# Head attention ahead of the first mixture in 32-row tiles, and values projected between the rows of the recurrent attention

## What is computed

```
# ffn0, ahead of its mixture: 16 heads of 8, batches of 64 tokens
Q = hs @ q_w + q_b; K = hs @ k_w + k_b; V = hs @ v_w + v_b
attn = softmax(Q[..., :8] @ K.T / sqrt(8)); ao = attn @ V
mla_out = concat(ao, 0) @ o_w + o_b          # the mixture's input
# attn1: 8 heads of 64
q, k, v = x @ Wq + bq, x @ Wk + bk, x @ Wv + bv
attn = softmax over heads of (q . k) * 64**-0.5
state = decay * state + (1 - decay) * attn * v     # over time
out = (q * state + sigmoid(q * aug)) @ Wo + bo
x = x + layernorm(out) * ln_scale + ln_bias
```

## Time and profile before

| | us |
|---|---|
| median of 3 runs | 1057.94 (1055.94 to 1062.13) |
| the profiled execution, its own time | 1060.44 |
| its span in the profile | 1058.7 |
| PE busy | 989.5 |
| DVE busy | 567.9 |
| ACT busy | 493.3 |
| POOL busy | 175.0 |

### The profile page before, as it was taken

How to read it: one execution, slowest core, us unless ns; L and a number is a source line. 1 busy time by engine, 2 the same in 40 slices (tenths; PEclk the granted TensorE clock), 3 DMA queues, 4 the chain that set the end, 5 groups by cost and what they waited for, 6 DMA issues and landing times. The chain is left out here.

```text
span 1058.7 us, 20860 instructions
## 1 busy us (share of the span) xinstructions
PE 989.5 (93%) x8710; PEld 814.5 (77%) x8710; DVE 567.9 (54%) x809; ACT 493.3 (47%) x696; POOL 175.0 (17%) x169
## 2 busy tenths in 40 slices
PE   8899999787789998899999999999999988959997
PEld 7788888664569995689999999999999966537554
DVE  4578776676634434665555555556564612176222
ACT  5677776252346653544545454544445421402221
POOL 2000000104304433011111111111111101320000
PEclk9899999899779999999999999999999999977999
DMA  5121110112013314021111111111130001988990
GB/s 163 45 66 45 48 45 3 27 34 64 1 51 92 96 40 159 4 78 40 41 41 40 40 40 40 40 40 40 40 119 0 1 1 33 292 287 222 300 303 20
DMA packets 55205, 81.47 MB, mean 77 GB/s; under 512 B 5073, under 2 KB 44578, under 8 KB 55138
## 3 DMA queue, kind: packets, MB, share of 16 engines
q1 hardware_dynamic: 55138, 80.49, 24.5%
HBM read 79.96 MB, written 0.52 MB: 76 GB/s over the span
## 5 line engine op out<-in xcount | busy, mean ns | idle before, releaser
L181 PE MATMUL ps<-f_pT_hi,f_cN_hi 128*128 128x256 f32 x512 | 145.4, 284 | 2.4 <-DVE f_pT_lo L1699 2.4
L181 PE MATMUL ps<-f_pT_hi,f_cN_lo 128*128 128x256 f32 x512 | 144.7, 283 | 0.0
L181 PE MATMUL ps<-f_pT_lo,f_cN_hi 128*128 128x256 f32 x512 | 144.7, 283 | 0.0
L1446 ACT ACTIVATE e_pr<-ps,e_negmax 128x1024 f32<-128x1024 f32 x64 | 71.5, 1118 | 129.8 <-DVE e_negmax L1451 127.5
L1699 DVE TENSOR_TENSOR f_pT_lo<-ps,f_pT_hi 128x1024 fp32r<-128x1024 f32 x64 | 78.3, 1224 | 81.7 <-ACT f_pT_hi L1647 81.6
L181 PE MATMUL ps<-e_cT_hi,e_qb_hi 128*128 128x512 f32 x256 | 105.6, 413 | 0.0
L1647 ACT CAST f_pT_hi<-ps 128x1024 fp32r<-128x1024 f32 x64 | 65.1, 1017 | 84.7 <-PE ps L1736 84.6
L404 DVE SCALAR_TENSOR_TENSOR a_u<-ps,a_floor,a_cap 128x1024 f32<-128x1024 f32 x64 | 79.2, 1279 | 46.7 <-PE ps L485 46.7
L181 PEld LDWEIGHTS ps<-f_pT_hi,f_cN_hi 128*128 128x128 f32 x512 | 97.8, 191 | 4.4 <-DVE f_pT_lo L1699 2.6
L181 PE MATMUL ps<-e_cT_hi,e_qb_lo 128*128 128x512 f32 x256 | 100.6, 393 | 0.0
L181 PE MATMUL ps<-e_cT_lo,e_qb_hi 128*128 128x512 f32 x256 | 99.9, 390 | 0.0
(11 more groups left out here) (373 smaller groups left out, 2039.2 us busy)
## 6 DMA issues: line engine op xcount, KB each, us to landing
k_w<-in_L_ffn_W SPq DMA_DIRECT2D x30, 1024.0 KB, 13.6
a_ctxT<-in_ctxT SPq DMA_DIRECT2D x16, 512.0 KB, 3.7
d_w<-in_L_ffn_w SPq DMA_DIRECT2D x32, 256.0 KB, 2.7
e_rawT<-in_ctxT SPq DMA_DIRECT2D x8, 1024.0 KB, 5.1
e_raw<-in_ctx SPq DMA_DIRECT2D x8, 1024.0 KB, 5.6
k_b<-in_L_ffn_b SPq DMA_DIRECT2D x14, 256.0 KB, 12.1
e_wq<-in_L_xattn_w_q SPq DMA_DIRECT2D x1, 1024.0 KB, 5.3
e_wk<-in_L_xattn_w_k SPq DMA_DIRECT2D x1, 1024.0 KB, 7.8
```

The lines of the kernel that those rows point to most:

```text
L181: last = nc.tensor.matmul(out, a[i], b[j], start=start and n == 0, stop=stop and n == 2, skip_group_check=skip)
L1446: nc.scalar.activation(pr[:, p % NPR, :], core.ps[p % 2][:], ACT.Exp, bias=negmax[:, p:p + 1], accum_out=total[:, p:p + 1]).then_inc(exp_r ...
```

## The change

In `ffn0`: the loads are reordered, K's first, each with its own semaphore; 15 warm matmuls instead of 12 and 4 more after the transposes; K and Q projected as before; the values in two halves between the scores; `kd` has 4 heads for each row (128x256) and is made by DVE alone; a score matmul takes 32 rows and 256 columns, 8 for each row tile in two sets of four with a semaphore between them; `pr` has four buffers; a column of ones beside the values gives the sum of the exponentials out of the same matmul; the bank pair of transposes is copied in two halves; v's bias is added while the output is evicted; transposes and output follow row tile by row tile. The exponential's table is loaded early, and ACT splits one part of the first expert's weights after each row tile.

In `attn1`: 16 warm matmuls; the sums of tile c follow K's projection of tile c+1; v's second to fourth tile stand between the transposes and rows; DVE waits for one v tile at a time; DVE makes the last of four `prod`; bo is put into PSUM by four matmuls ahead of `wo`; statistics are taken from PSUM, scaling by lns is folded into the subtraction of the mean and rstd into the addition to x.

```diff
@@ ffn0
+                for dst, src, done in ((wk, a["L0_ffn_k_w"], k_in), (wq, a["L0_ffn_q_w"], q_in),
+                                       (wv, a["L0_ffn_v_w"], v_in)):
+                for dst, src, done in ((bk, "k_b", k_in), (bq, "q_b", q_in), (bv, "v_b", o_in), (bo, "o_b", o_in)):
...
 @block.gpsimd
-                pool.wait_ge(qk_ready, 1)
-                for b in range(B // 2, B):
-                    nc.gpsimd.tensor_tensor(kd[:, b, :, :], bc(kT[:, b * T:b * T + T], 1, H),
-                                            bc(headmask[:], 2, T), ALU.mult).then_inc(kd_pool, 1)
...
 @block.scalar
                 for j in range(TT):
-                    if j == 1:
-                        mixture.prepare_scalar(act)
...
+                    turned(j)
+                    if j + 1 < TT:
+                        exponentials(j + 1)
+                    if j >= 1:
+                        attended(j - 1)
+                    mixture.experts.high(act, 0, (0, 2, 1, 3)[j])
+                projected(0)
+                attended(3)
+                projected(1)
...
 @block.vector
+                def keys(b):
+                    V.tensor_tensor(kd[:, b, :, :], bc(kT[:, b * T:b * T + T], 1, HR), bc(headmod[:], 2, T),
+                                    ALU.mult).then_inc(kd_ready, 1)
+                def weighted(j):
+                    dve.wait_ge(o_psum, j + 1)
+                    o = core.bank(6)[:, 0:H * (HD + 1)].rearrange("p (h d) -> p h d", d=HD + 1)
+                    step(V.reciprocal(sm[:, j, :], o[:, :, HD]))
+                    V.tensor_tensor(ao[:, j, :, :], o[:, :, 0:HD], bc(sm[:, j, :], 2, HD), ALU.mult
+                                    ).then_inc(o_ready, 1)
...
-                        step(V.reduce_sum(sm[:, i, :], pr[:, i % 2, :, :], AX))
...
+                for b in range(B):
+                    keys(b)
+                for j in range(TT):
+                    shifted(j)
+                for j in range(TT):
+                    weighted(j)
...
 @block.tensor
+                    for second, tiles in enumerate((((0, 0), (0, 2), (1, 1), (1, 3)), ((0, 1), (0, 3), (1, 0), (1, 2)))):
+                        if second == 1:
+                            pe.wait_ge(s_first, NR * (j + 1))
+                        for g, r in tiles:
+                            b, rows = 2 * j + g, slice(ROWS * r, ROWS * r + ROWS)
+                            cols = slice(HR * T * r, HR * T * r + HR * T)
+                            t.matmul(core.ps[j % 2][T * g:T * g + T, cols], qT[rows, b * T:b * T + T],
+                                     kd[rows, b, :, :].rearrange("p h t -> p (h t)"), start=True, stop=True
+                                     ).then_inc(s_psum if second else s_first, 1)
...
+                def attend(j):
                     if j >= 1:
                         pe.wait_ge(o_ready, j)
...
+                norm.tensor(pe, 15, 4)
+                pe.wait_ge(k_in, 32)
+                project(2, wk).then_inc(k_psum, 1)
...
+                for j in range(TT):
+                    transposes(j)
+                    if j == 0:
+                        scores(3)
+                    attend(j)
+                    if j >= 1:
+                        turn(j - 1)
+                output(0)
+                turn(TT - 1)
+                output(1)
@@ attn1
...
-            norm.tensor(pe)
+            norm.tensor(pe, 16)
...
+            for c in range(HC):
+                project(wk, 4, k_psum, prod_ready, c, c + 1)
+                if c >= 1:
+                    sums(c - 1)
+            sums(HC - 1).then_inc(s_psum, 1)
...
+            for j in range(TT):
+                t.matmul(Y(j), share[:], bo[:], start=True, stop=False, skip_group_check=True)
...
 @block.gpsimd
-            for c in range(HC):
+            for c in range(HC - 1):
                 pool.wait_ge(state, c + 1)
                 g.tensor_tensor(prod[:, c, :], u[:, c, :], sig[:, c, :], ALU.add).then_inc(o_ready, 1)
...
 @block.vector
+            V.tensor_tensor(prod[:, HC - 1, :], u[:, HC - 1, :], sig[:, HC - 1, :], ALU.add).then_inc(last_ready, 1)
...
-                step(V.tensor_tensor(y[:, j, :], core.bank(Y_BANKS[j])[:, 0:D], bo[:], ALU.add), j == TT - 1)
...
+                step(V.scalar_tensor_tensor(y[:, j, :], Y(j), core.meanvar[:, j, 0:1], lns[:], ALU.subtract, ALU.mult),
+                     False)
+            norm2.vector_rstd(dve, step)
             dve.wait_ge(x_biased, 1)
-            V.tensor_tensor(x[:], x[:], y[:], ALU.add).then_inc(x_out, 1)
+            for j in range(TT):
+                V.scalar_tensor_tensor(x[:, j, :], y[:, j, :], core.rstd[:, j:j + 1], x[:, j, :], ALU.mult, ALU.add
+                                       ).then_inc(x_out, 1)
```

More of the change, by code:

```diff
@@ new lines, in turned, with attended @@
+                def turned(j):
+                    for half in range(2):
+                        act.wait_ge(pT_psum, 2 * j + half + 1)
+                        if j >= 2 and half == 0:
+                            act.wait_ge(o_psum, j - 1)
+                        A.copy(pT[:, j % 2, 512 * half:512 * half + 512], core.bank(4 + half)).then_inc(pT_ready, 1)
+                def attended(j):
+                    act.wait_ge(oT_psum, j + 1)
+                    A.activation(aoT[:, j * P:(j + 1) * P], core.bank(7)[:, j * P:(j + 1) * P], ACT.Identity,
+                                 bias=bv[:]).then_inc(oT_ready, 1)
@@ new lines, in projected, with values @@
+                def projected(half):
+                    cols = slice(NT // 2 * half, NT // 2 * half + NT // 2)
+                    for c in range(DC):
+                        act.wait_ge(m_psum, DC * half + c + 1)
+                        last = A.activation(mlaT[:, c, cols], core.bank(c)[:, cols], ACT.Identity, bias=bo[:, c:c + 1])
+                        if half == 1:
+                            last.then_inc(mlaT_ready, 1)
+                def values(b):
+                    act.wait_ge(v_psum, b + 1)
+                    for g in range(2):
+                        half = slice(T * g, T * g + T)
+                        A.copy(vd[half, 4 * b:4 * b + 4, :, g, 0:HD], vp(b)[half, :, :, g, :]).then_inc(vd_ready, 1)
@@ new lines, in _ @@
+                norm.tensor(pe, 15, 4)
+                pe.wait_ge(k_in, 32)
+                project(2, wk).then_inc(k_psum, 1)
+                pe.wait_ge(q_in, 32)
+                project(3, wq).then_inc(q_psum, 1)
+                pe.wait_ge(v_in, 16)
+                for b in range(B // 2):
+                    last = values(b)
+                    if b == B // 4 - 1:
+                        pe.wait_ge(q_ready, 1)
+                        scores(0)
+                last.then_inc(v_psum, 1)
@@ new lines, in _ @@
+                scores(1)
+                for b in range(B // 2, B):
+                    last = values(b)
+                last.then_inc(v_psum, 1)
+                pe.wait_ge(o_in, 48)
+                scores(2)
+                for j in range(TT):
+                    transposes(j)
+                    if j == 0:
+                        scores(3)
+                    attend(j)
+                    if j >= 1:
+                        turn(j - 1)
+                output(0)
+                turn(TT - 1)
```

302 lines of the change are left out of this document (151 added, 151 removed).

## The result

The changed kernel takes 1029.77 us (median, 1029.22 to 1030.17), the kernel before 1057.82 on the same chip: a ratio of 0.9712 [0.9682, 0.9741]. In a later set of rounds the two came to 1029.77 and 1057.77, 0.9728 [0.9692, 0.9764]. The profiled execution took 1030.17 us, its span is 31.3 us shorter than before, while the medians differ by 28.1. Of the 3.2 us between the two, 2.2 lie in the executions that were profiled (2.6 above the median before, 0.4 after) and 1.0 outside the spans.

The account below looks back on a forecast made before the run. The prediction took chains of waits between engines, none of them full, to bound both stages. Savings of 14.3 us (head attention) and 8.5 us (`attn1`), 22.8 off the median 1057.94, gave 1035 us, range 1028 to 1043.

Parts of the forecast that it names:

- The row tiles: Head attention's last three row tiles: low clock from 268 on, 5.5 us each, 15.5 us together; whole stage 14.3 us less.
- the rival of the high clock: Clock stays high between the head attention's row tiles: 3.2 us each, stage 21.8 us less, launch 1028 us; chance 0.25.
- The start: Head attention's start: K's projection begins 1.5 us earlier, and the K and Q projections take 3.5 us, 1.8 less.
- kd: Head attention: DVE alone makes eight smaller kd products of 0.41 us each, all done 3.3 us after K.
- Scores: Head attention: a row tile's 16 score records take 1.3 us, with 0.9 and 3.5 kept as bounds.
- The rival of row groups one by one: Score row groups do not overlap: 3.5 us a row tile instead of 1.3, launch 1042 us; chance 0.15.
- PE's queue: Head attention: PE's work from 254.6 through the first small matmuls takes 11.0 us plus 0.5 for semaphores, ending at 266.1.
- attn1: Recurrent attention: savings of 1.7, 3.1, 0.8, 0.6 and 2.3 us, together 8.5 us less; 6.8 if the clock falls.
- The last sum: End of `attn1`'s loop: the last sum moves from POOL (1.26 us) to DVE (near 0.7), 0.6 us less.
- The tail: End of `attn1`: statistics, means, products, reciprocal chain and additions take 6.4 us instead of 8.7, 2.3 less.
- The last block: Last block: its start 8 us earlier costs nothing, as a hole in the DMA traffic leaves room for the expert weights.

Follow-up runs that it names:

- wholecopy: The changed kernel with ACT copying a row tile's transposes in one piece again instead of two halves; 1041.08 us, executed once.
- filled: `wholecopy` plus four warm matmuls ahead of the small matmuls of the second to fourth row tile; 1033.53 us, executed once.
- gap: The changed kernel with the head attention's old start: 12 warm matmuls, K's projection waiting for the last small load; 1031.70 us, executed once.
- fullrows: The changed kernel with kd of 16 heads again, made half on POOL, and scores over all 128 rows; 1039.58 us, executed once.
- serialtiles: The changed kernel with a row tile's scores in four sets of one row group each, a semaphore between sets; 1047.83 us, executed once.
- recur_only: The changed kernel with the old `ffn0`, so only the recurrent attention is changed; 1047.69 us, ratio 0.9869.
- attn_only: The changed kernel with the old `attn1`, so only the head attention is changed; 1037.47 us, ratio 0.9778.
- attn_warm16: `attn_only` with 16 instead of 12 warm matmuls ahead of the transposes in `attn1`; 1041.44 us, executed once.
- recur_warm12: `recur_only` with 12 instead of 16 warm matmuls ahead of the transposes in `attn1`; 1056.44 us, executed once.
- warm12: The changed kernel with 12 instead of 16 warm matmuls ahead of the transposes in `attn1`; 1028.81 us, executed once.
- poolprod: The changed kernel with the last sum of `attn1`'s loop given back from DVE to POOL; 1029.50 us, executed once.

## Why the prediction was right and where it was wrong

**The row tiles: the step that failed.** "So I take the low clock from 268 on: 3 x 5.5 less 1.0 for the part before = 15.5." The clock stayed at 1.00, the row tiles took 3.2 us each, and the stage lost 20.9 us, not 14.3; this was the rival of the high clock, given 0.25 (21.8 there). The reason given was the fall soon after the last scores before. But the small matmuls there stood behind a wait of 1.10 us for the whole copy, and the change shortens just this wait by copying halves. My sum had no term for this wait at either clock, and so I carried the old clock over although its cause was being removed. `wholecopy` and `filled` show cause and price: 7.1 us.

The rival's sum was in part luck. It gives a row tile 1.09 + 2.01 us and a turn, with no wait. The measured 3.2 are 1.04 + 0.67 of waiting + 1.39 and a turn: the missing wait and the small matmuls, taken 0.6 too long, cancel.

**The start.** K's projection started 0.06 us behind xnT, as forecast, and 6.3 us behind its block's start (forecast 6.0). The two projections took 3.6 us (forecast 3.5), and `gap` prices cover and early load at 2.8 us; the sum had 1.5 + 1.8.

**kd.** The eight products have a mean of 417 ns and take 2.77 us from first to last, as one starts before the other ends in the records; forecast 0.41 and 3.3. `fullrows` shows the alternative's price, 8.0 us with the clock that fell there. That DVE and POOL slow each other was read from two kinds of operation, and no run here has the large product on one engine alone.

**Scores.** 1.49 us a row tile, forecast 1.3 (0.9 to 3.5). A set of eight records takes 0.66 us, where one by one at 0.22 they would take 1.8. The wait on the semaphore between the sets costs 0.17 us. The Trainium skill (TensorE: Matmul & The Clock Gate, Part 3) says that different row groups run at once, and the trace agrees: a set over four row groups takes 0.66 us, and with one row group at a time the scores take 2.87 us instead of 1.49. The prediction says that the written sets keep row groups out of the same PSUM bank. They do so only within one half of the output rows: in a set, row groups 0 and 1 write the same bank at once, each in its own half of the rows, and they ran side by side. The rival of row groups one by one (3.5 us, 1042) is out; its form was built in `serialtiles` (2.87 at full clock).

**PE's queue.** The first small matmuls ended 22.1 us behind the block's start (265.0), forecast 22.0 (266.1 on an axis where the block starts at 244.1). They take 1.42 us, not 2.0. The 2.01 of the kernel before ended in the low clock; in `recur_only` the same train took 1.83 at full clock. The rest is in their order: the changed queue turns more often between the two halves of the output rows, and behind such a turn its records start some 27 ns apart instead of 58. The last eviction came 35.7 us behind the block's start; the rival's sum said 34.7.

**attn1.** 8.4 us less, forecast 8.5. Q's clock: 7.13 instead of 8.8, 1.7 as forecast. The four warm matmuls keep it in the old `attn1` (`attn_only` against `attn_warm16`) and in `recur_only` against `recur_warm12`; in the changed kernel itself `warm12` had 7.13 without them, so there they are a cause that is not shown. The maximum came 24.0 us behind the block's start, before 28.9: 4.9 less, forecast 1.7 + 3.1. DVE's first product 5.7 less, forecast 5.6. The loop 12.3 us, unchanged. The last sum was mis-sized: from the loop's end to the tail's first operation it is 1.92 us, before 2.12, so 0.2 less instead of 0.6 (`poolprod`: 0.23), since PE's last output matmuls stand behind it on either engine. The tail took 6.2 us, forecast 6.4, and 8.7 before.

**The last block.** From `attn1`'s last addition to the span's end it took 105.3 us, before 106.0, without waits on weights: the term of nothing held. In the profiles with the changed `attn1` and no warm matmuls behind it this length is from 104.2 to 105.8 us, so the 0.7 is within chance.

**The sum.** The part that was wrong is 6.6 us in one term. Of the span the saving is 31.3 us where 22.8 were forecast; the other 1.9 us are the earlier start of the stage (1.2), the last block (0.7) and 0.1 between, less 0.1 in `attn1`. The forecast took the saving off the median; by medians it is 28.1.

## What to carry to other kernels

When a change shortens a wait of PE, ask first whether that wait is what had let the clock fall: a wait shorter by 0.6 us or less in three row tiles brought 7.1. Don't carry a clock level from the old trace to the new one; carry the idle times beside it. And fill an idle time only where PE ends last: in front of a wait for DVE the full clock bought 0.4 us or less, and 36 warm matmuls, sized wrongly by two, held the next block up by 3 us. Look at what stands behind, too: in the old `attn1` the full clock for Q was followed by a fall behind narrow matmuls, and the block got longer.

## What the runs showed of the hardware

- Eight records of 32 rows x 64 columns of weights and 256 columns of data, spread over four row groups and both column halves, took 0.66 us, and four of one row group 0.65; 16 of them took 1.49 in two sets of the first kind and 2.87 in four of the second (`serialtiles`).
- In `serialtiles` the clock fell with PE busy for 3.72 of 4 us on such narrow work, and in `attn_warm16` behind 32 records of 8 columns with PE busy for 3.00 of 3 us: the busy row of the page does not show all that bears on the clock.
- In row tiles of 3.2 us a wait of 0.67 us left the clock at 1.00; a wait of 1.25 us (`wholecopy`) brought it to 0.50, where it stayed to the stage's end; 1.1 us ahead of Q's transposes did so for Q's projection in three of four profiles.
- DVE's `kd` product took 2.5 us beside POOL's, and a fourth of its size, with POOL idle, 0.35 from one start to the next (417 ns each by the records).
